# Four reorderings in a fused mixer and expert kernel: tokens' weights, half a modulation, filler products, gathered gates

## The chip, the cores and the metric

The kernel runs on one core of one Trainium2 chip. The metric is the device time in microseconds. Three runs of the kernel before gave 544.57, 546.89 and 544.63, so the median is 544.63.

## The reference, cut to what matters

One block of a modulated network on x of shape (4, 512, 512), all in float32:

```python
mod = (silu(c) @ wmod).reshape(4, 6, 1, -1)            # sa, ca, ga, sb, cb, gb per batch
h = layernorm(x) * (1 + ca) + sa
x = x + ga * attn(h)       # causal depthwise conv (4 taps), B/C/delta products, softplus,
                           # scan h_t = dA_t * h_(t-1) + Bu_t, output product, + D * conv
h = layernorm(x) * (1 + cb) + sb
logits = h @ w_router.T; probs = softmax(logits)       # 2 experts, every token goes to one
a = square(where(h@w_fc >= 0, h@w_fc, 0.5 * h@w_fc))
out = top_probability * (a @ w_proj of the chosen expert)
x = x + gb * out
```

## The kernel before, in words

There are two stages. The **mixer** (0 to about 148 us) works through four batches of 512 tokens, b = 0 to 3. The **expert stage** (to the end) works on the 2048 tokens sorted by expert in 17 blocks of 128 rows, which make up five units of 4, 4, 4, 3 and 2 blocks (`UNITS`; `FIRST` = 0, 4, 8, 12, 15 is the first block of each). It runs over eight blocks of hidden columns (`hb` = 0 to 7). Each engine has a queue of its own, written out by hand in program order, and semaphores tie them. No planner orders anything. So an instruction that waits holds up all that stands behind it on the same engine.

Batch b in the mixer, with the helpers of the code: VectorE takes the statistics of a row (`stats1`), ScalarE guesses the reciprocal root (`guess1`), VectorE mends it (`newton1`), ScalarE normalizes (`normalize1`). TensorE turns the rows over (`transposes1`, L1006), ScalarE multiplies and shifts on the way out of the accumulator (`modulate1`, L695) and starts the convolution (`last_tap`, L703). VectorE adds the other three taps (`conv`, L1359). TensorE computes `delta_product`, `C_product` (L1030), `B_product` (L1038), `state_product` (L1048) and `spread_delta` (L1024). ScalarE's `exp_minus_abs` (L711, L713) and `log_part` with VectorE's `softplus_residue` (L1368, L1370) and `softplus` make delta, and ScalarE's `decay` (L723, L725) copies it and exponentiates it. `scan` on VectorE (L1381 to L1388) needs delta, decay and the products. TensorE adds `skip_product` (L1063) and `state_output` (L1067), VectorE adds the residual (`residual`, L1397).

The second half of a batch is the router: `row_stats2` and `stats2` (statistics), `guess2` on ScalarE, `margin_products` on VectorE (four fused multiply-and-sum instructions, L1421, which raise `s_q`), `newton2`, `margins`. The last writes the mask `m1` (L1435), on which TensorE's `prefix` (L1072, L1073) and GpSimd's `candidates` (L555) wait, and the margin `al`, of which ScalarE takes the exponential (`margin_exp`, L744), behind the four instructions of `normalize2` (L739). One batch later, behind the scan, VectorE computes `ranks`, `permutations` (L1454) and `top_weight` of the batch before: two small instructions (L1458, L1461) that turn the exponential into each token's weight, 1 / (1 + e). GpSimd then scatters positions, tokens and weights of that batch to memory with four indirect transfers (L586). Before those it waits for `top_weight` (`s_tw`), and behind them stands its work on the next batch, `candidates` first. TensorE's `permuted_block` (L1091) and ScalarE's `place` (L777, L781) write the sorted rows.

In the expert stage TensorE multiplies without a break (L1180, L1201 for the first product, L1232 for the second) and VectorE accumulates. In its last block of columns, `hb` = 7, GpSimd does this in order: it gathers each row's `gb` gate (`gather_gb`, L598), adds x's own rows into blocks 8 to 16 (`add_own`, L605, each waiting for a block that VectorE has prepared, `s_pre`, L1678), waits until all those have landed, adds blocks 0 to 7 into the output (`add_rows`, L613) and stores blocks 8 to 16 (`put_rows`, L620). Each store waits for its block (`s_or`). The gates of blocks 4 to 7 (unit index 1) are needed by VectorE's `finish_rows(1)` (L1662). VectorE's last steps are `last_products` (L1686) and `last_sums` (L1693).

Of the kernel before, what the change touches and what calls it, by code (L numbers as in the profile page):

```python
# [35 lines left out]
TJ = L // P  # L36
# [3 lines left out]
UNITS = (4, 4, 4, 3, 2)  # L40
# [64 lines left out]
def build(nc, x, cT, wmod, wx, win, wout, conv_w, conv_b, A_log, Dvec, router_rows, wffn, out):  # L105
    with ExitStack() as ctx:
# [406 lines left out]
        def _(pool):  # L513
# [88 lines left out]
            def add_own(n):  # L602

                pool.wait_ge(s_pre, n - DIRECT + 1)
                pool.indirect_dma_start(out=acc[:, n, :], out_offset=None, in_=out,  # L605
                                        in_offset=bass.IndirectOffsetOnAxis(ap=sorted_meta[:, n, 1:2].bitcast(I32), axis=0),
                                        bounds_check=TOK - 1, oob_is_err=False, compute_op=ALU.add).then_inc(s_own[n - DIRECT], 16)
# [35 lines left out]
                add_own(n)  # L643

            pool.wait_ge(s_h[HM - 1], NU * (NHB - 1))
            for n in GATES[CH:]:
                gather_gb(n)
            for n in range(FIRST[3], NSUB):
                add_own(n)

            for n in range(NSUB - DIRECT):
                pool.wait_ge(s_own[n], 16)
# [7 lines left out]
        def _(act):  # L660
# [158 lines left out]
            mod_row_copy(4)  # L819
            normalize1(2)  # L820
            mod_row_copy(5)
            decay(1)
            guess2(0)
            modulate1(2, (0, 1))
            guess1(3)
            modulate1(2, (2, 3))
            last_tap(2, range(KT))
            normalize2(0)
            margin_exp(0)
# [123 lines left out]
        def _(pe):  # L953
# [112 lines left out]
            def state_output(b, j):  # L1066
                pe.matmul(out_bank[j][:, :], hs[:, P * j:P * j + P], woutg[b][:, :], start=False, stop=True).then_inc(s_y, 1)  # L1067

            def prefix(b):
                pe.wait_ge(s_m1, b + 1)  # L1070
                pe.wait_ge(s_x2, TJ * (b + 1))
                pe.matmul(pO[0][:, 0:TJ], before[:, :], m1[:, :], start=True, stop=True).then_inc(s_pf, 1)  # L1072
                pe.matmul(pO[0][:, TJ:2 * TJ], ones[:, :], m1[:, :], start=True, stop=True).then_inc(s_pf, 1)  # L1073
# [42 lines left out]
            for b in range(NB):  # L1116
# [44 lines left out]
                    transposes1(b + 2, (2, 3))  # L1161
                if b == 0:
                    delta_product(2)
                prefix(b)
            PARTS = ((0, 0), (0, 1), (1, 0))
            W, XS, A = (Whi, Wlo), (XShi, XSlo), (ahi, alo)
# [148 lines left out]
        def _(dve):  # L1315
# [253 lines left out]
            for b in range(NB):  # L1569
                nxt = b + 1 < NB  # L1570
                scan(b)
                if b == 0:
                    for n in range(NB):
                        out_weights(n)
                else:
                    ranks(b - 1)
                    permutations(b - 1)
                    if b == NB - 1:
                        assign_first()
                    top_weight(b - 1)  # L1580
                    if b == NB - 1:
                        prepare_rest()
                taps = {}
# [16 lines left out]
                if nxt:  # L1600
# [6 lines left out]
                    for n in range(TJ):  # L1607
                        row_stats2(b, n)
                stats2(b)
                if b == 0:  # L1610
                    router_row(False)
                    stats1(3)
# [65 lines left out]
                    dve.scalar_tensor_tensor(acc[:, n, :], acc[:, n, :], sorted_meta[:, n, 0:1], gb_row[n][:, :], ALU.mult,  # L1678
                                             ALU.mult).then_inc(s_pre, 1)

            def last_products(u, banks):
                for s in range(UNITS[u]):
                    n = FIRST[u] + s
                    dve.wait_ge(s_yy, NSUB * (NHB - 1) + n + 1)
                    dve.wait_ge(s_pre, n - DIRECT + 1)
                    dve.scalar_tensor_tensor(gb_row[n][:, :], yP[banks[s]][:, :], sorted_meta[:, n, 0:1], gb_row[n][:, :],  # L1686
                                             ALU.mult, ALU.mult).then_inc(s_yu, 1)
# [68 lines left out]
                low(NHB - 1, u)  # L1756
                finish_rows(u - 1)
            twice(1, NHB - 1, 3)
            last_products(2, range(WIDE))
            low(NHB - 1, 3)  # L1760
            last_sums(range(FIRST[2], FIRST[2] + 2))
            twice(1, NHB - 1, NU - 1)
            last_sums(range(FIRST[2] + 2, FIRST[3]))
            last_low()
            last_products(3, (0, 1, 2))
            last_sums(range(FIRST[3], FIRST[4]))
            last_products(4, (3, 0))
            last_sums(range(FIRST[4], NSUB))


# [33 lines left out]
```

## Time and profile before

| | |
|---|---|
| median of three runs | 544.63 us |
| the profiled execution, its own time | 547.68 us |
| its span, first to last instruction | 545.9 us |
| TensorE busy | 502.0 us, 92% of the span |
| VectorE busy | 345.7 us, 63% |
| ScalarE busy | 259.4 us, 48% |
| GpSimd busy | 158.4 us, 29% |
| mean granted TensorE clock | 0.958 |

The shares are averages over the two stages. The mixer takes a quarter of the span, and its work passes from engine to engine. The expert stage takes the rest, and nearly all of it is TensorE. What a reordering is worth has to be read inside its own stretch: in the timeline (one line for each run of equal instructions, with the idle time before it and what ended that) and in the windows (busy time of each engine in a stretch and the clock granted to TensorE).

### The profile page before, as it was taken

Reading aid. Unit: us, or ns where it says so; the run is one execution under the profiler, and the core shown is the slowest. Engines: PE = TensorE matmul, PEld = TensorE weight load, DVE = VectorE, ACT = ScalarE, POOL = GpSimd, SP = SyncE. Lnnn points to the kernel's source line nnn. Section 1 sums busy time; section 2 is a strip of 40 time slices with the busy share of each in tenths; the row PEclk is TensorE's granted clock in tenths of the full one; section 3 lists DMA queues with packets and bytes.
Section 4 is the critical chain, followed back from the end, with each engine's and each line's share of the span. In section 5 each row is a group of like instructions: output and inputs, shape, how many; then the busy total and the mean of one; then the engine's idle time right before and its main releaser. Section 6 shows DMA issues by size and latency. Waiting matters only on the chain.

```text
span 545.9 us, 7958 instructions
## 1 busy us (share of the span) xinstructions
PE 502.0 (92%) x2408; PEld 392.8 (72%) x2408; DVE 345.7 (63%) x730; ACT 259.4 (48%) x524; POOL 158.4 (29%) x204
## 2 busy tenths in 40 slices
PE   7899789987397999999999999999999999999990
PEld 1464365736276888898888888888888888988880
DVE  4579999699998575454445354545454534668781
ACT  1774295956785633443443354344345334433220
POOL 1100021122243510330150033034004304868673
PEclk9899969998697999999999999999999999999995
DMA  8931242220051004130022022002102300468692
GB/s 294 424 133 57 103 152 77 79 77 2 1 162 72 4 3 156 30 126 2 1 79 79 1 78 80 1 1 94 64 1 78 118 1 6 117 112 182 78 167 98
DMA packets 15730, 46.31 MB, mean 85 GB/s; under 512 B 5223, under 2 KB 5223, under 8 KB 12344
## 3 DMA queue, kind: packets, MB, share of 16 engines
q1 hardware_dynamic: 10600, 34.71, 17.9%
q0 software_dynamic: 5072, 10.79, 9.6%
q8 instruction: 41, 0.67, 0.5%
q14 instruction: 17, 0.14, 0.1%
HBM read 37.30 MB, written 8.71 MB: 84 GB/s over the span
## 4 chain that ended last, share of the span: by engine, by line
PE 75%; DVE 13%; ACT 4%; issue 3%; DMA 1%; ACTq 1%; POOL 1%; DVEq 0%; SPq 0%; POOLq 0%
PE bank L1232 34%; PE bank L1201 32%; DVE xc L1359 3%; ACT XSfull L777 2%; DVE st L1404 1%; DVE st L1341 1%; DMA x_in<-x 1%; PE bank L1030 1%; PE bank L1038 1%; DVE res L1397 1%; PE bank L1063 1%; PE bank L1006 1%; DVE eabs L1421 1%; PE bank L1067 1%; DVE hs L1387 1%
## 5 line engine op out<-in xcount | busy, mean ns | idle before, releaser
L569 POOL TENSOR_TENSOR Wlo<-raw,Whi (+1 forms) x60 | 76.6, 1307 | 228.0 <-ACT Whi L921 219.9
L1656 DVE TENSOR_TENSOR acc<-acc,bank 128x512 f32<-128x512 f32 x110 | 74.8, 687 | 57.2 <-PE bank L1232 57.2
L1232 PE MATMUL bank<-Whi,ahi 128*128 128x512 f32 x268 | 105.5, 394 | 4.3 <-DVE alo L1646 4.3
L1640 DVE TENSOR_TENSOR twice_h<-twice_h,bank 128x512 f32<-128x512 f32 (+2 forms) x80 | 48.2, 605 | 95.6 <-ACT twice_h L892 95.5
L1201 PE MATMUL bank<-XShi,Wlo 128*128 x304 | 108.1, 356 | 0.0
L1201 PE MATMUL bank<-XSlo,Whi 128*128 x304 | 108.0, 355 | 0.0
L1201 PE MATMUL bank<-XShi,Whi 128*128 x304 | 108.0, 355 | 0.0
L1232 PE MATMUL bank<-Wlo,ahi 128*128 128x512 f32 x268 | 105.5, 394 | 0.0
L1232 PE MATMUL bank<-Whi,alo 128*128 128x512 f32 x268 | 105.3, 393 | 0.0
L901 ACT ACTIVATE ahi<-twice_h 128x512 fp32r<-128x512 f32 (+2 forms) x78 | 44.6, 572 | 120.0 <-PE bank L1232 119.9
L892 ACT ACTIVATE twice_h<-bank 128x512 f32<-128x512 f32 (+2 forms) x78 | 41.4, 533 | 86.9 <-PE bank L1201 76.2
L1201 PEld LDWEIGHTS bank<-XSlo,Whi 128*128 128x128 f32 x304 | 57.3, 189 | 7.5
L1201 PEld LDWEIGHTS bank<-XShi,Whi 128*128 128x128 f32 x304 | 57.3, 189 | 7.5
L1201 PEld LDWEIGHTS bank<-XShi,Wlo 128*128 128x128 f32 x304 | 57.3, 188 | 6.8
L1232 PEld LDWEIGHTS bank<-Whi,ahi 128*128 128x128 f32 x268 | 51.0, 190 | 14.9 <-issue 4.7
L1232 PEld LDWEIGHTS bank<-Whi,alo 128*128 128x128 f32 x268 | 50.9, 190 | 10.8
L1232 PEld LDWEIGHTS bank<-Wlo,ahi 128*128 128x128 f32 x268 | 50.9, 190 | 10.2
L1646 DVE TENSOR_TENSOR alo<-a_full,ahi 128x512 fp32r<-128x512 f32 (+2 forms) x78 | 45.4, 612 | 0.0
L902 ACT ACTIVATE a_full<-twice_h 128x512 f32<-128x512 f32 (+2 forms) x78 | 43.3, 556 | 0.0
L1359 DVE SCALAR_TENSOR_TENSOR xc<-hT,cw,xc 128x512 f32<-128x512 f32 x48 | 33.6, 742 | 2.5 <-ACT xc L703 2.2
L777 ACT ACTIVATE XSfull<-bank,cols 128x128 f32 (+1 forms) x64 | 24.1, 460 | 20.0 <-PE bank L1091 17.7
L921 ACT ACTIVATE Whi<-raw 128x512 fp32r<-128x512 f32 x56 | 30.5, 616 | 0.0
(201 smaller groups left out, 570.1 us busy)
## 6 DMA issues: line engine op xcount, KB each, us to landing
raw<-wffn SPq DMA_DIRECT2D x16, 1024.0 KB, 5.1
wm<-wmod SPq DMA_DIRECT2D x6, 1024.0 KB, 12.8
out<-res SPq DMA_DIRECT2D x4, 1024.0 KB, 4.5
x_in<-x SPq DMA_DIRECT2D x3, 1024.0 KB, 12.4
ga_bc<-ga_rows SPq DMA_DIRECT2D x4, 256.0 KB, 3.7
x<-x SPq DMA_DIRECT2D x1, 1024.0 KB, 5.1
bc<-router_rows_scaled SPq DMA_DIRECT2D x4, 256.0 KB, 3.5
wx_sb<-wx SPq DMA_DIRECT2D x1, 514.0 KB, 8.6
```

The source lines that it names most:

```text
L569: pool.tensor_tensor(Wlo[:, hb % 2, c, :], raw[:, c, :], Whi[:, hb % 2, c, :].bitcast(F32), ALU.subtract).then_inc(s_wlo, 1)
L777: act.activation(XSfull[:, k, bass.ds(first, P)], place_bank[b][j][:, P * k:P * k + P], ACT.Identity, bias=cols[:, 4, k, b:b + 1], scale=c ...
L892: act.activation(twice_h[:, m, 0:w], hP[(par + u) % 2][m][:, 0:w], ACT.Relu).then_inc(s_relu[m], 1)
L901: act.activation(ahi[:, m, 0:w], twice_h[:, m, 0:w], ACT.Square, scale=0.5).then_inc(s_ah[m], 1)
L902: act.activation(a_full[:, m, 0:w], twice_h[:, m, 0:w], ACT.Square, scale=0.5).then_inc(s_af[m], 1)
L921: act.activation(Whi[:, 1 - par, c, :], raw[:, c, :], ACT.Copy).then_inc(s_whi, 1)
L1201: mm = pe.matmul(hP[(par + u) % 2][m][:, c0:c1], W[wp][:, par, 2 * e + k // 2, o:o + P], XS[xp][:, k, bass.ds(start_row[u] + c0, c1 - c0)] ...
L1232: mm = pe.matmul(yP[bank_of[s]][:, :], ahl[ap][:, m, P * s:P * s + P], W[wp][:, par, 4 + 2 * experts[s] + m, :], start=(m == 0 and n == 0) ...
L1359: ins = dve.scalar_tensor_tensor(xc[:, b % 2, k, :], hT[b % 2][:, k, tap:tap + L], cw[:, k, tap:tap + 1], xc[:, b % 2, k, :], ALU.mult, AL ...
L1640: dve.tensor_tensor(twice_h[:, m, 0:w], twice_h[:, m, 0:w], hP[(par + u) % 2][m][:, 0:w], ALU.add).then_inc(s_q2[m], 1)
L1646: dve.tensor_tensor(alo[:, m, 0:w], a_full[:, m, 0:w], ahi[:, m, 0:w].bitcast(F32), ALU.subtract).then_inc(s_al2[m], 1)
L1656: dve.tensor_tensor(acc[:, n, :], acc[:, n, :], yP[s][:, :], ALU.add).then_inc(s_yu, 1)
```

## The change

```diff
@@ GpSimd, last block of columns
             pool.wait_ge(s_h[HM - 1], NU * (NHB - 1))
-            for n in GATES[CH:]:
+            for n in range(1, FIRST[1]):
                 gather_gb(n)
             for n in range(FIRST[3], NSUB):
                 add_own(n)
+            assert GATES[CH - 1:] == tuple(range(DIRECT))
+            for n in range(FIRST[1], DIRECT):
+                gather_gb(n)
@@ ScalarE
             mod_row_copy(5)
+            modulate1(2, (0, 1))
+            guess2(0)
             decay(1)
-            guess2(0)
-            modulate1(2, (0, 1))
+            modulate1(2, (2, 3))
             guess1(3)
-            modulate1(2, (2, 3))
             last_tap(2, range(KT))
@@ TensorE
+            def keep_rate(b, count):
+                pe.wait_ge(s_q, TJ * b + 2)
+                pe.wait_ge(s_x2, TJ * (b + 1))
+                for n in range(count):
+                    pe.matmul(pO[1][:, :], ident[:, :], wout_sb[:, :], start=True, stop=True)
...
                 if b == 0:
                     delta_product(2)
+                    keep_rate(b, 3)
+                if b == 2:
+                    keep_rate(b, 2)
                 prefix(b)
@@ VectorE
                     if b == NB - 1:
                         assign_first()
-                    top_weight(b - 1)
                     if b == NB - 1:
                         prepare_rest()
...
                 stats2(b)
+                if b > 0:
+                    top_weight(b - 1)
                 if b == 0:
@@ VectorE, the end
-            last_products(3, (0, 1, 2))
-            last_sums(range(FIRST[3], FIRST[4]))
-            last_products(4, (3, 0))
+            last_products(3, (0, 1, 2), (0, 1))
+            last_sums((FIRST[3],))
+            last_products(3, (0, 1, 2), (2,))
+            last_sums((FIRST[3] + 1, FIRST[3] + 2))
+            last_products(4, (3, 0), (0, 1))
             last_sums(range(FIRST[4], NSUB))
```

`last_products` gets a third argument, the rows of the unit that it works on; the call for unit 2 passes all four. The products of `keep_rate` are 128 x 128 by 128 x 512 in float32, and nothing reads what they write.

## Rows read from the trace of the kernel before

**Rows 1.** The head of the page.

```profile
span 545.9 us, 7958 instructions
```

**Rows 2.** VectorE's waits, 0 to 170 us: total, times, longest.

```profile
DVE den L1458 <- ACT eal L744: 2.9, 1, 2.9
```

**Rows 3.** Timeline, batch 1's scan and after: start, duration, instruction, [idle before <-releaser].

```profile
93.55 1.50 ACT L777 ACTIVATE XSfull<-bank,cols 128x128 f32 x4 [2.76 <-PE bank L1091]
...
98.80 0.58 ACT L723 ACTIVATE delta<-bank 128x512 f32<-128x512 f32 x1
...
99.41 0.69 DVE L1381 TENSOR_TENSOR eabs<-delta,bank 128x512 f32<-128x512 f32 x1 [1.42 <-ACT delta L723]
...
107.10 0.26 ACT L711 ACTIVATE eabs<-bank 128x128 f32<-128x128 f32 x1
107.23 0.17 DVE L1458 TENSOR_SCALAR den<-eal 128x4 f32<-128x4 f32 x1 [2.93 <-ACT eal L744]
...
107.43 0.18 DVE L1461 RECIPROCAL meta<-den 128x4 f32<-128x4 f32 x1
...
110.15 0.22 DVE L1368 TENSOR_SCALAR w<-eabs 128x128 f32<-128x128 f32 x1
```

**Rows 4.** Timeline of TensorE, 68 to 89 us.

```profile
68.42 1.33 PE L1006 MATMUL bank<-ident,z 128*128 128x128 f32 x8 [2.44 <-ACT hT L695]
...
73.31 0.59 PE L1072 MATMUL bank<-m,before 128*128 128x4 f32 x2 [1.90 <-DVE m L1435]
...
74.18 5.47 PE L1063 MATMUL bank<-diag,xc 128*128 128x128 f32 x24
...
85.08 3.60 PE L1030 MATMUL bank<-hT,wx_sb 128*128 128x512 f32 x8
```

**Rows 5.** Windows: stretch, busy of PE, PEld, DVE, ACT, POOL, then PEclk.

```profile
69.50:71.00 1.50, 1.50 (x35) 0.91 (x33) 1.31 (x6) 1.50 (x3) 0.00 (x0) 0.69 1.26 392
```

**Rows 6.** Timeline of GpSimd after batch 0's token weights.

```profile
108.38 1.46 POOL L586 DMA_INDIRECT sorted_rows<-meta,posI  x1 [4.24 <-issue]
...
113.74 0.21 POOL L574 COPY meta<-tokbat 128x8 int32<-128x8 int32 x1
```

**Rows 7.** Timeline, batch 2's mask and batch 3's first residual.

```profile
127.16 0.39 PE L1072 MATMUL bank<-m,before 128*128 128x4 f32 x2 [2.82 <-DVE m L1435]
...
134.19 0.69 DVE L1397 TENSOR_TENSOR res<-bank,x 128x512 f32<-128x512 f32 x1
```

**Rows 8.** The chain that ended last: start, us, what.

```profile
167.32 8.16 PE bank L1232 x24
...
180.92 5.44 PE bank L1232 x24
```

**Rows 9.** Timeline of GpSimd, 488 us to its last transfer.

```profile
488.50 1.00 POOL L598 DMA_INDIRECT gb_row<-gb_rows,sorted_meta  x1 [0.30 <-issue]
...
497.56 1.57 POOL L605 DMA_INDIRECT acc<-out,sorted_meta  x1 [0.30 <-issue]
...
511.17 1.59 POOL L613 DMA_INDIRECT out<-acc,sorted_meta  x1 [4.35 <-DMA acc<-out,sorted_meta]
...
526.84 1.03 POOL L620 DMA_INDIRECT out<-acc,sorted_meta  x1 [0.30 <-issue]
...
537.83 0.98 POOL L620 DMA_INDIRECT out<-acc,sorted_meta  x1 [0.30 <-issue]
```

**Rows 10.** The 17 gate gathers, line L598.

```profile
DMA to landing us min/median/max: 3.7/4.4/6.9
```

**Rows 11.** Timeline of VectorE in the last block of columns.

```profile
492.46 3.39 DVE L1678 SCALAR_TENSOR_TENSOR acc<-acc,sorted_meta,gb_row 128x512 f32<-128x512 f32 x5
...
514.22 2.73 DVE L1662 SCALAR_TENSOR_TENSOR acc<-acc,sorted_meta,gb_row 128x512 f32<-128x512 f32 x4
...
523.63 1.29 DVE L1693 TENSOR_TENSOR acc<-acc,gb_row 128x512 f32<-128x512 f32 x2
...
532.80 1.28 DVE L1693 TENSOR_TENSOR acc<-acc,gb_row 128x512 f32<-128x512 f32 x2
```

More of the change, by code:

```diff
@@ L1679, in prepare_rows, with last_products @@
                                              ALU.mult).then_inc(s_pre, 1)
-            def last_products(u, banks):
-                for s in range(UNITS[u]):
+            def last_products(u, banks, rows):
+                for s in rows:
                     n = FIRST[u] + s
@@ L1758, in _ @@
             twice(1, NHB - 1, 3)
-            last_products(2, range(WIDE))
+            last_products(2, range(WIDE), range(WIDE))
             low(NHB - 1, 3)
```

## The prediction, made before the changed kernel ran

> **What bounds the kernel now.** I read the page, then the chain that ended last, then VectorE's waits, then the timeline of the two stretches that the diff touches. The page gives the span, 545.9 us [rows 1]; the profiled execution took 547.68, 1.8 more, and the median of the runs is 544.63, 3.05 below it. From 167 us on the chain of waits is TensorE in runs of 24 products, 5.44 us each [rows 8], up to its last product near 531.7. Nothing in the diff touches that, so the middle of the kernel only moves with what lies ahead of it. Two stretches are left.
>
> In the mixer the bound is VectorE: it has work almost without a gap from 40 to 167 us, and what counts are its few waits. The longest one that the diff touches is 2.9 us for ScalarE's exponential [rows 2]. The timeline shows its place: behind batch 2's scan and ranks, `top_weight(1)` starts at 107.23 after 2.93 us of idling, and the convolution of batch 3 stands behind it. A second wait, 1.42 us, is for delta at 99.41 [rows 3].
>
> At the end the bound is not VectorE or TensorE, whatever the chain says, but GpSimd's queue. VectorE's last sum ends at 532.80 + 1.28 = 534.1 [rows 11]; GpSimd issues its last store at 537.83, with only the fixed 0.30 us of issue before each [rows 9]. That stream of 17 transfers runs without a real gap from 511.17, and there it had waited 4.35 us for the own rows to land.
>
> **The change part by part.**
>
> *Tokens' weights behind the next statistics.* In the loop's step b = 2 the two instructions leave a place where they waited. Removed there: 2.93 us of waiting and 107.61 - 107.23 = 0.38 us of work. Both instructions come back behind `stats2`, with the exponential long there, so the 0.38 is gained up to that point and given back after it. In b = 1 and b = 3 there was no wait and only the 0.38 moves. In b = 3 it is gained for what counts: between the old place and the new one stand `prepare_rest`, the residual at 134.19 [rows 7] and `stats2(3)`, whose result releases ScalarE's last `guess2`, two `place` blocks behind it and with them the start of the expert stage.
>
> *What is late next.* Without the wait VectorE starts the four taps at once and wants `exp_minus_abs(3)` behind them, which ended at 107.10 + 0.57 = 107.7 (two short instructions) [rows 3]. VectorE's taps would end at 110.15 - 2.93 - 0.38 = 106.8. So if ScalarE keeps its times the new wait is 0.9 and the gain at that point 110.15 - 107.75 = 2.4. It is 3.3 if ScalarE is earlier by 0.9 or more.
>
> *Filler products and half a modulation.* These are what makes ScalarE earlier. TensorE idled 2.44 us before 68.42 because it needed ScalarE's modulation, and 1.90 before 73.31 for the mask. Its clock fell to 1.2 GHz between those (0.69 mean in 69.5 to 71.0 [rows 5]) and the 24 short products of L1063 took 5.47 us [rows 4]. At full clock they take half of that, 2.7. So 2.7 us, with the outputs behind them about 3.0, are lost by TensorE from 74 on, and it works without a gap from there to 98. ScalarE waits for it at 93.55 (2.76 us for a permuted block [rows 3]) and runs without a gap from there to 98.80, 13.6 us in all to 107.10. With the modulation's first half in the free time before 66.02, the transposes of the second half follow at 66.0 rather than 68.4, `delta_product(2)` ends near 69.2, and three fillers follow. One float32 product of 512 columns is two of the eight records in 3.60 us, so 0.9, three cost 2.6 and end at 71.8, before the mask at 73.3: no cost. The gap left is 1.5. I take it that the clock holds: two gaps of 2.44 and 1.90 close together brought it down, and one of 1.5 is less than either; the lower end is that it falls as before. Then TensorE's permuted block comes 3 us sooner, `guess2(1)` follows VectorE's statistics, `decay(2)` goes from 98.80 to about 95.9, the 1.42 wait disappears, and ScalarE is 2.9 early at 107.10, so no new wait. Mixer gain: 1.42 + 2.93 + 0.38 = 4.7. If the fillers do nothing: 2.4. If the modulation delays a decay: it cannot, `decay(1)` waits for TensorE until 66.02 anyway; the two instructions (1.43) and `guess2(0)` (0.4) fit ahead of it.
>
> The two fillers of b = 2 (1.7 us) lie in the 2.82 us before 127.16 [rows 7]. At this place VectorE reaches its residual at 134.19 some 1 us after TensorE has delivered, so a full clock gives it nothing; it lets ScalarE place two blocks in time for the shift by 4.7. Worth 0 alone, at the least -0.2 if they overrun the mask.
>
> *GpSimd in the mixer.* The four scatters of a batch now come behind `stats2`, in front of `candidates` of the next batch. From the weights at 107.61 to the next copy at 113.74 they take 6.1 us [rows 3, 6]. In b = 1 `stats2` ends at 93.1: the candidates come at 93.1 + 6.1 + 0.8 = 100.0; `ranks` wants them at 102.71 - 1.4 = 101.3. Slack 1.3, and 1.0 in b = 2 (weights at 117.9, candidates 124.9, ranks 126.0). Cost 0; two slow transfers, 0.5 each more, would still fit.
>
> *Start of the expert stage.* The first run of 24 products took 8.16 instead of 5.44, because TensorE had idled and was at the low clock: 2.7 lost [rows 8]. It idles as long in the new kernel. Where in its run the clock comes back I can't tell, so 0, with both ends: between 1 us less and 1 us more.
>
> *Gates of blocks 4 to 7 later.* Seven gathers took 488.50 to 497.56, 1.3 each, then five own rows 1.87 each to 506.8, then the wait to 511.17 [rows 9]. Now three gathers end at 492.4. The first own row waits for VectorE: 492.46 + 0.68, and 0.8 from there to the transfer (as from 107.61 to 108.38 [rows 3, 6]), so 493.9. Five: 503.2. Four gathers: 508.5. The own rows, landed at 508 at the latest (506.8 - 503.2 = 3.6 before 511.17 - 0.6), no longer delay. The 17 transfers start at 508.8, 2.3 earlier. `finish_rows(1)` at 514.22 needs the gates: the last is issued at about 507.4 and lands 3.7 to 6.9 later [rows 10], 511.1 to 514.3. No cost. But the stream now meets VectorE: the first store, 526.84 - 2.3 = 524.5, needs a sum that ends at 523.63 + 0.65 = 524.3 and starts 0.8 later, 525.1. So 1.7 remain. The split of `last_products(3)` puts block 12's sum at 529.7 rather than 530.4, against a store wanted at 530.5: it saves 0.8 that the shift would otherwise have lost again. The last store can't be before 534.1 + 0.8 = 534.9 and comes by the stream at 536.1. Tail gain 1.7; bounds 0 (if transfers and not issues hold the stream) and 2.9 (537.83 - 534.9).
>
> **Sum.** 4.7 + 1.7 + 0 = 6.4 on the profiled execution: 547.68 to 541.3. The median lies 3.05 lower. If the timed runs are like the profiled one but for a constant, that gives 538.2. If the clock did not fall at 70 us in the timed runs, the 1.42 wait was not there, and 5.0 remain: 539.6. I take the middle, 539.0.
>
> The Trainium skill ("TensorE: Matmul & The Clock Gate", Part 1) says that the point at which the clock changes is not tied to the kernel's start and differs from run to run. By that rule the second of these two readings holds in part of the runs, and the fillers are worth nothing in those: it speaks for 539.6. The spread of the three runs, 2.3 us, goes with it; a single trace can't show it.
>
> **Rivals.**
> - *ScalarE takes over as the bound.* The clock falls anyway (the gaps before 73.3 are not filled tightly enough) or was never low in timed runs and something else holds ScalarE. For: ScalarE has no idle time from 93.55 to 107.7 [rows 3]. Against: 3 us of slack come with the clock. The mixer gives 2.4, the tail 1.7: 544.6 - 4.1 = 540.5.
> - *The tail gives nothing.* The transfers themselves hold the stream and not their issue, so a burst that starts earlier ends no earlier. For: the eight adds are (526.84 - 511.17) / 8 = 1.96 apart. Against: the stores behind them are (537.83 - 526.84) / 8 = 1.37 apart, little over one issue of 0.98 and 0.30 [rows 9]. 544.6 - 4.7 = 539.9, and with the rival above 542.2, which is within 0.5% of before.
> - *Slower: the gates come too late.* `finish_rows(1)` stands ahead of VectorE's next `twice`, which releases TensorE's next products. If the four gathers land behind the own rows' adds, every us past 514.3 is one us of TensorE. It turns the sum of 6.4 negative only if the last lands later than 520.7, 13 us after its issue; the worst seen is 6.9 [rows 10]. At 16 us it would give 544.6 + 2.7 = 547.3.
> - *The weights' scatters hold `ranks`*: each us over the slack of 1.0 to 1.3 costs one us in each of two batches; at 1.5 us over, 539.0 + 3 = 542.
>
> **How the numbers follow.** Forecast, by its two readings 538.2 and 539.6: 0.28 and 0.27. ScalarE bound, 540.5: 0.18. No tail gain, 539.9: 0.10. Both, or the scatters over their slack, 542 to 544: 0.13. Slower: 0.04. The range takes the first four to 542.2 and downwards the 1 us of the expert stage's start and the tail's 2.9: 536.8. The measurement can tell 0.5%, 2.7 us, from no change: under 541.9 is faster, 0.82; same 0.14; slower 0.04.
>
> **What would show it.** In the changed profile: no wait of VectorE at L1458; `exp_minus_abs(3)` without a VectorE wait at L1368 (wrong if some 0.9 stands there); a full clock from 69 to 138 us; L1063 x24 in about 2.7 us; no wait for delta at L1381; L1442 with no wait for `cand`; the start of L1232 near 162.6; GpSimd's first L613 about 2.3 earlier relative to TensorE's last product, its last L620 about 1.7. The prediction is wrong if the first L1232 comes less than 2 us earlier, or if a wait for a gate shows at L1662.

## The result: 542.8 against 546.2 us, faster, by less than forecast

In the first comparison, on one chip, the changed kernel took 542.8 us in the median of 9 runs (541.03 to 543.46), the kernel before 546.18 (9 runs, 544.57 to 549.05). The ratio is 0.9936, 95% interval 0.9913 to 0.9959. A second comparison on another chip gave 542.41 (540.36 to 543.07) against 545.8, ratio 0.9928, interval 0.9907 to 0.9949. So 3.4 us are gained, faster by 0.6%. The forecast was 539.0 with a range up to 542.2: the direction was right, the time is 0.6 us outside the range. The starting point moved too: the forecast counted from 544.63, the median of three runs of the kernel before, and its nine runs here have 546.18. One execution of a later experiment (fill_order_gates_back) took 865.4 us at a granted clock of 0.559, and its ratio is without it.

The profiled execution of the changed kernel took 543.34 (span 541.6, mean granted clock 0.969), that of the kernel before 547.68 (span 545.9): 4.3 less where 6.4 were forecast. First VectorE and ScalarE around batch 1's scan (timeline, as [rows 3]):

```profile
96.38 0.58 ACT L727 ACTIVATE delta<-bank 128x512 f32<-128x512 f32 x1
...
98.36 0.68 DVE L1395 TENSOR_TENSOR eabs<-delta,bank 128x512 f32<-128x512 f32 x1
...
104.68 0.26 ACT L715 ACTIVATE eabs<-bank 128x128 f32<-128x128 f32 x1
105.97 0.22 DVE L1382 TENSOR_SCALAR w<-eabs 128x128 f32<-128x128 f32 x1
```

L1395 is the old L1381 and L1382 the old L1368. Delta stood at 98.80 and stands at 96.38; VectorE wanted it at 98.3 and no longer waits. The weights' two instructions and their wait of 2.93 have left this place, and the taps end at 105.97 instead of 110.15. ScalarE's two instructions that they need next were finished 0.7 us earlier (at 105.29), so no new wait took the place of the old one.

TensorE (timeline, as [rows 4]; L1078 are the unread products):

```profile
66.26 1.04 PE L1010 MATMUL bank<-ident,z 128*128 128x128 f32 x8
...
69.56 2.84 PE L1078 MATMUL bank<-wout_sb,ident 128*128 128x512 f32 x6
73.76 0.39 PE L1083 MATMUL bank<-m,before 128*128 128x4 f32 x2 [1.36 <-DVE m L1449]
74.23 2.97 PE L1067 MATMUL bank<-diag,xc 128*128 128x128 f32 x24
```

The transposes are 2.2 earlier with no wait ahead of them, the two gaps of 2.44 and 1.90 have become one of 1.36, and the 24 short products take 2.97 instead of 5.47. The mask itself is 0.44 later than before, since the whole execution entered this stretch 0.44 later. The first projection of the expert stage and the last transfers (chain of waits, then GpSimd's timeline, as [rows 8, 9]):

```profile
163.92 8.50 PE bank L1246 x24
```

```profile
506.01 1.62 POOL L613 DMA_INDIRECT out<-acc,sorted_meta  x1 [0.30 <-issue]
...
522.07 1.04 POOL L620 DMA_INDIRECT out<-acc,sorted_meta  x1 [1.17 <-DVE acc L1708]
...
533.48 0.98 POOL L620 DMA_INDIRECT out<-acc,sorted_meta  x1 [0.30 <-issue]
```

The projection starts 3.40 earlier and its first run takes 0.34 longer; TensorE's last product is 3.06 earlier (528.24 against 531.30). The wait of 4.35 ahead of the first L613 is gone, and one of 1.17 for VectorE's sum stands ahead of the first L620. The last store comes 4.35 earlier: 5.24 after TensorE's last product instead of 6.53, so the tail (from TensorE's last product to the last store) gave 1.29. In all the profiled execution gained 3.40 at the projection, less 0.34 in its first run, plus 1.29 in the tail: 4.35.

### The profile page after: what moved, and what is told of

It is laid out like the page before. It is cut to its first block, busy times and chain, and to the rows that moved or that the text cites. A ratio compares the mean times of both kernels' runs of the same rounds, so it can differ in the third digit from the quotient of the medians.

```text
span 541.6 us, 7980 instructions
## 1 busy us (share of the span) xinstructions
PE 501.2 (93%) x2418; PEld 390.0 (72%) x2418; DVE 346.4 (64%) x730; ACT 259.8 (48%) x524; POOL 159.3 (29%) x204
## 4 chain that ended last, share of the span: by engine, by line
PE 71%; DVE 18%; issue 4%; ACT 3%; DMA 1%; ACTq 1%; DVEq 0%; POOL 0%; SPq 0%; POOLq 0%
PE bank L1246 34%; PE bank L1215 33%; DVE xc L1373 4%; DVE st L1418 2%; DVE res L1411 2%; DVE st L1355 1%; DMA x_in<-x 1%; DVE eabs L1435 1%; DVE hs L1401 1%; ACT XSfull L781 1%; PE bank L1194 1%; PE bank L1034 1%; PE bank L965 1%; PE bank L1052 1%; PE bank L1042 1%
## 5 line engine op out<-in xcount | busy, mean ns | idle before, releaser
L586 POOL DMA_INDIRECT sorted_rows<-meta,posI x16 | 16.8, 1050 | 50.7 <-issue 50.7
```

Source lines behind the costliest of these rows:

```text
L586: pool.indirect_dma_start(out=meta_dram, out_offset=bass.IndirectOffsetOnAxis(ap=posI[:, b % 2, j:j + 1], axis=0), in_=meta[:, b % 2, j, : ...
```

## The experiments

All kernels compute the whole reference. Each comparison has the kernel before on the same chip; medians of different chips are not compared with each other.

**The kernel before, a second time.**

> The kernel before, unchanged, run as a kernel of its own, to see another trace of it and its spread. Theory A (the forecast's error was that I carried a fixed 3.05 us from the profiled execution to the median): the executions of this same program differ by 2 to 4 us, and a trace of a fast one (about 544.6) shows the TensorE clock full near 70 to 80 us, L1063 x24 in about 3.0 instead of 5.47 us and no 1.42 us wait for delta at L1381. Theory B (the profile was typical and single parts of the change give less when timed): the trace looks as before, clock low from 70 to 80, and all times lie within 1 us of each other.

Measured: 545.91 (544.68 to 549.26), ratio 1.0011 (0.9982 to 1.004). Its profiled execution (548.62, clock 0.957) shows the same waits as the first, 2.9 at L1458 and 1.4 at L1381. Its twelve executions are of two kinds: eight of 544.7 to 546.2 at a clock of 0.960 to 0.969, four of 548.5 to 549.3 at 0.957. Both profiles of the kernel before caught the low-clock one. So the distance from profile to median depends on which kind the profile caught, and that reopened the last step of the prediction.

**The tokens' weights at their old place.**

```diff
+                    top_weight(b - 1)
...
-                if b > 0:
-                    top_weight(b - 1)
```

> The changed kernel with the tokens' weights back at their old place, right behind the ranks. Theory A: with the products' clock kept, ScalarE delivers the exponential at 104.6, VectorE reaches it at 103.3, so the wait returns at about 1.4 us and with the 0.3 of work the mixer is 1.7 us longer: 544.5 against the changed kernel's 542.8. Theory B (the wait removed was the 2.93 of the old trace whatever else changed): 3.3 us longer, 546.1, as slow as the kernel before.

Measured: 542.96 (540.38 to 545.46), ratio 0.9945 (0.9915 to 0.9976). The wait is back (VectorE's timeline):

```profile
98.17 0.68 DVE L1395 TENSOR_TENSOR eabs<-delta,bank 128x512 f32<-128x512 f32 x1
...
105.82 0.17 DVE L1472 TENSOR_SCALAR den<-eal 128x4 f32<-128x4 f32 x1 [2.77 <-ACT eal L748]
...
108.75 0.22 DVE L1382 TENSOR_SCALAR w<-eabs 128x128 f32<-128x128 f32 x1
```

From L1395 to L1382 it is 10.58 us against 7.61 in the changed kernel, 2.97 more, and 2.03 of it are left at the first projection (165.95 against 163.92). But the two profiles don't differ in this part alone. This one has the unread products and the gap of 1.35 behind them as the changed kernel has, and still its clock fell between 73 and 79 us (the window has 0.72), and the 24 short products took 4.51 instead of 2.97:

```profile
73.56 0.39 PE L1083 MATMUL bank<-m,before 128*128 128x4 f32 x2 [1.35 <-DVE m L1449]
...
74.03 4.51 PE L1067 MATMUL bank<-diag,xc 128*128 128x128 f32 x24
```

Where the clock is full there, in the profiles of fill_tw_back and fill_order_tw_back below, the wait is 1.85 and 1.86 and L1395 to L1382 takes 9.67 and 9.66. So this part is worth 2.06 at that point at a full clock, and the 2.97 hold some 0.9 of the clock. The ratio is only 0.0009 (0.5 us) above the changed kernel's: four of the twelve executions took 540.4 to 540.8 at a clock of 0.977. Something pays out in some executions and not in others, as large as the part itself.

**No unread products.**

```diff
-                    keep_rate(b, 3)
-                if b == 2:
-                    keep_rate(b, 2)
```

> The changed kernel without the five unread products. Theory A: the clock falls near 70 us in part of the executions, and in those batch 1 runs 2.4 to 3 us later on TensorE and VectorE waits 1 to 2 us more; in the others nothing is lost. Median 1 us longer, 543.8, spread wider. Theory B: the modulation ahead of the decay alone keeps TensorE busy enough, 542.8.

Measured: 545.15 (543.35 to 546.15), ratio 0.9983 (0.9957 to 1.0009), the clock 0.956 to 0.966 in all executions. TensorE and VectorE's waits:

```profile
66.06 1.04 PE L1010 MATMUL bank<-ident,z 128*128 128x128 f32 x8
...
73.55 0.59 PE L1083 MATMUL bank<-m,before 128*128 128x4 f32 x2 [4.13 <-DVE m L1446]
74.43 4.72 PE L1067 MATMUL bank<-diag,xc 128*128 128x128 f32 x24
```

```profile
DVE w L1379 <- ACT eabs L717: 0.8, 1, 0.8
```

With the modulation moved alone the two gaps join into one of 4.13, the clock falls in it, the products take 4.72, and VectorE meets a late exponential: 0.8, the size that the prediction gave for that case (0.9). The rest of the change without this part gives 0.2%, in an interval that includes no change. This is the rival "ScalarE takes over as the bound", made to happen.

**Unit 2's gates in the old order.**

```diff
-            for n in range(1, FIRST[1]):
+            for n in GATES[CH:]:
...
-            for n in range(FIRST[1], DIRECT):
-                gather_gb(n)
```

> The changed kernel with all seven gates gathered ahead of the own rows, as before. Theory A: GpSimd waits some 4.3 us again for the own rows, the last 17 transfers start 2.1 us later relative to TensorE's last product, the last store 1.3 us later: 544.1. Theory B (the transfers and not their issue set the end): 542.8, and the last store lands as far behind TensorE's last product as in the changed kernel, 13.3 us from 528.24 to the end.

Measured: 544.13 (541.74 to 545.17), ratio 0.9965 (0.994 to 0.9989). In its profile the last L620 starts at 533.07 and the last product at 526.49, 6.58 apart, against 5.24 in the changed kernel and 6.53 in the kernel before. The tail's part is 1.3. The median is no measure of it here: it depends on the mix of executions, which spread over 3.4 us.

**Unread products wherever TensorE idles ahead of the expert stage.** Eight more around the last prefix sums, four ahead of the first projection, to take the clock out of the comparison; then the same with one part of the change taken back, and on the kernel before.

```diff
+                if b == NB - 1:
+                    pe.wait_ge(s_x2, TJ * NB)
+                    for n in range(6):
+                        pe.matmul(pO[1][:, :], ident[:, :], wout_sb[:, :], start=True, stop=True)
...
+                if b == NB - 1:
+                    for n in range(2):
+                        pe.matmul(pO[1][:, :], ident[:, :], wout_sb[:, :], start=True, stop=True)
...
+            for n in range(4):
+                pe.matmul(place_bank[NB - 1][0][:, :], ident[:, :], wout_sb[:, :], start=True, stop=True)
```

> The changed kernel with 12 more unread products: six before the last prefix, two behind it (TensorE waits 6.7 and 2.3 us there) and four before the first second-product of the expert stage (4.0 us). Theory A (where the clock falls differs from execution to execution, and that is what spreads the runs and what my sum left out): the clock stays full from 10 us to the last product, the first 24 products of L1246 take 5.44 instead of 8.5 us, the first product of the expert stage 1.85 instead of 3.77, and the median falls by 3 to 5 us to 538 to 540 with a spread under 1 us. Theory B (the spread has another source, such as when the first loads land): the median falls by no more than 3 and the spread of some 2.5 us stays.

> As fill_both, with the tokens' weights back at their old place. With the clock held in every wait only this step differs. Theory A (the trace's wait of 2.8 us for the exponential is real and on the path): 2.0 us slower than fill_both, as the first second-product came at 165.95 against 163.92 in the two traces. Theory B (timed runs say it gives nothing: 542.96 against 542.8): equal to fill_both within 0.5 us.

> As fill_both, with the gates gathered in the old order. Theory A: 1.3 us slower than fill_both, since GpSimd's stream of the last 17 transfers starts 2.1 us later and VectorE takes back 0.8. Theory B (transfers set the end): equal.

> The kernel before with all unread products (those of the change and the twelve of fill_both) and nothing else of the change. Theory A: the clock costs the kernel before up to 8 us in its slow executions and 3 in its fast ones; this gives 542.5 with a spread under 1 us, and the rest of the change (weights 2.0, gates 1.3, the modulation 0.5) is what lies between it and fill_both, 3.8 us. Theory B: the fillers give the kernel before less than 1.5 us, 544.5 or more.

Measured: fill_both 543.7 (543.4 to 545.17), ratio 0.9981 (0.996 to 1.0002); without the weights' move 544.51, 0.9995 (0.9972 to 1.0018); without the gates' move 545.04, 1.0003 (0.998 to 1.0025); the kernel before with all unread products 545.59, 1.0022 (1.0 to 1.0045). The clock rose to 0.974 to 0.988 and ten of fill_both's twelve executions lie within 0.6 us, so in this kernel the clock carried most of the spread. But a higher clock made the kernel no faster. Where it went is in GpSimd's and VectorE's groups, 149 to 165 us (busy us, mean ns, idle before). First the changed kernel:

```profile
L569 POOL TENSOR_TENSOR Wlo<-raw,Whi 128x512 fp32r<-128x512 f32 x4 | 5.5, 1406 | 8.3 <-ACT Whi L760 8.3
L1637 DVE TENSOR_TENSOR XSlo<-XSfull,XShi x4 | 3.6, 961 | 0.5 <-issue 0.5
```

then fill_both:

```profile
L569 POOL TENSOR_TENSOR Wlo<-raw,Whi 128x512 fp32r<-128x512 f32 x4 | 6.3, 1617 | 6.2 <-ACT Whi L760 6.2
L1648 DVE TENSOR_TENSOR XSlo<-XSfull,XShi x4 | 6.6, 1705 | 0.5 <-issue 0.5
```

VectorE's four low halves take 1705 ns each instead of 961. GpSimd's four, also a subtraction of two operands from the SBUF, run beside them and rise from 1406 to 1617. The first projection of fill_both came at 166.94, behind 3.67 us of unread products, against 163.92. The new theory: the two engines slow each other when both work on two SBUF operands, and work that arrives earlier falls into the overlap. (One more trace of this batch bears on the clock: in fill_gates_back the 24 short products took 4.58 in spite of the unread products ahead of them, as in tw_back.)

**The overlap forbidden.** GpSimd's halves wait until VectorE's of batch 2 are written: one line, added to fill_both, to the changed kernel, and to fill_both with a part taken back.

```diff
+                    pool.wait_ge(s_xlo, KT * 2)
                     pool.wait_ge(s_wlo, CH // 2)
                     for c in range(CH // 2, CH):
```

> The twelve further unread products stay, and GpSimd's low halves of batch 2's second group of blocks (L569, x4) wait until VectorE's low halves of batch 2 (L1648, x4) are written. Theory A (the two engines slow each other when both work on two operands in the SBUF): the group L1648 falls from 6.6 us to about 2.5, the first token projection comes about 4.1 us earlier than the 166.7 of the same kernel without the order, near 162.6, and the median is about 543.7 - 4.1 = 539.6. Theory B (VectorE's low halves are late for another reason, and GpSimd's halves are themselves needed at once): L1648 keeps over 4 us or L569 ends later by as much as L1648 gains, the first projection stays near 166.7, and the median stays within 0.8 of 543.7.

> The changed kernel with that one order added (GpSimd's L569 x4 behind VectorE's L1637 x4 of batch 2), no further unread products. Theory A: L1637 takes 2.5 us instead of 3.6, the first projection comes about 1 us earlier than 163.9, the median is about 541.7, and the spread between executions with a high and a low granted clock stays. Theory B: nothing is gained or up to 1 us is lost, since GpSimd's halves end later: 542.8 to 543.8.

> As fill_order, but the token weights are found ahead of the statistics again (the old place). If the clock and the order are settled by the two additions, the difference to fill_order is what that part of the change is worth by itself: the exponential wait of 2.8 comes back ahead of the statistics (L1382 of the changed kernel), less what the idle engine did in it, so +2.0 by the shift of the first projection in the changed kernel and the one without this part (163.92 against 165.95). If the part's value is hidden by a transfer or by ScalarE, +0.5 or less.

> As fill_order, but unit 2's gates are gathered ahead of the rows again (the old order). Theory: the tail's 1.3 us (4.35 of L613's and L620's shift less 3.06 of PE's last product) come back, +1.3 over fill_order. Rival: the tail is set by the last GpSimd rows whatever the gathers do, +0.4 or less.

Measured, all on one chip (the kernel before 543.57): fill_order 540.64 (539.5 to 542.69), ratio 0.9937 (0.9909 to 0.9965); order_only 540.8 (538.84 to 542.19), 0.9939 (0.9911 to 0.9967); fill_order_tw_back 541.97, 0.9955 (0.9934 to 0.9976); fill_order_gates_back 541.6, 0.9958 (0.9935 to 0.9981). The groups in fill_order, the second one VectorE's over a window with three more of them:

```profile
L569 POOL TENSOR_TENSOR Wlo<-raw,Whi 128x512 fp32r<-128x512 f32 x4 | 5.0, 1294 | 9.1 <-DVE XSlo L1649 9.1
L1649 DVE TENSOR_TENSOR XSlo<-XSfull,XShi x7 | 4.4, 685 | 0.5 <-issue 0.5
```

685 and 1294 ns each alone, 1705 and 1617 together: theory A. The first projection is at 163.06 instead of 166.94, 3.9 earlier as expected (4.1; 0.4 of it was gained ahead of this stretch, so 3.4 are the order's), and against the kernel before the same unread products give 0.6% instead of 0.2%. The Trainium skill ("GPSIMD Engine Reference", 1. Specifications) lists the SBUF interfaces as shared with VectorE, with contention for instructions with two SBUF inputs. By that rule these two groups must meet, and the traces agree; the page has no price, and here it is 1.0 us per VectorE instruction of 128x512 and 0.3 per GpSimd instruction.

With the order settled the parts can be read between kernels of one chip: the weights' move 1.33 (expected 2.0), the gates' move 0.96 (expected 1.3). No interval was taken of these two differences, and the ranges overlap. For the directions stands that fill_order's four fastest executions (539.5 to 539.9) lie 1 us below the fastest of either kernel with a part taken back (540.99, 540.97). The 2.0 came from profiles with different clocks, as said above.

The clock isn't settled, though. fill_order's other four executions took 541.4 to 542.7, at 0.977 to 0.986 instead of 0.987 to 0.990. That these are a kind of their own is likely and not shown: fill_order's profile is of a fast one. But the profile of fill_order_tw_back caught a slower execution (543.15, clock 0.984), and in it the eight records of the four unread products ahead of the projection took 5.37 instead of 3.67 us, as in the profile of fill_tw_back. The chain that ended last shows them there:

```profile
161.28 5.37 PE bank L1324 x8
```

So the products that were to keep the clock full ran in part at the low one themselves, and the projection waited for them.

**The last four.** To separate what was still open: the changed kernel again; the combination that the runs pointed to (the eight products around the last prefix sums and the order); the order on the kernel before; and the modulation alone taken back, whose edit stands here. The order is the same line, now behind the wait for `s_wlo`.

```diff
-            modulate1(2, (0, 1))
-            guess2(0)
...
-            modulate1(2, (2, 3))
+            guess2(0)
+            modulate1(2, (0, 1))
...
+            modulate1(2, (2, 3))
```

> The changed kernel unchanged, as the measure for the three others on this chip. Theory: its median stays 2.5 to 3.5 under the kernel before, and its executions spread over 4 us with the granted clock, from about 540.5 at 0.977 to 545 at 0.965.

> The changed kernel with eight of the unread products around the last prefix sums (none ahead of the first projection) and with GpSimd's L569 x4 behind VectorE's low halves of batch 2. Theory A (both engines slow each other, and the four products ahead of the projection delay it: in fill_order it began at 163.06 behind 3.67 of them, in order_only at 162.17 without): the projection begins near 161.5 at the full clock, the median is 3 under after_again and the spread under 2 us. Theory B (the order alone gives all of it): as order_only, 2 under after_again, and no less spread.

> The kernel before with GpSimd's L569 x4 behind VectorE's low halves of batch 2, nothing of the change. In the kernel before one of the four instructions L1622 took 1.79 instead of 0.68, so theory A expects 1.1 us less in executions with a low clock there and up to 4 us less in those with a high one: a median 1 to 2 under the kernel before. Theory B (the overlap matters only once the change has moved the work): under 0.5.

> The changed kernel with batch 2's modulation in its old place (both halves behind the decay, the guess ahead of it). By the prediction's step the delta wait of 1.42 ahead of L1395 comes back and every later row of the mixer is about 1.4 later: +1.4 over after_again. Rival: the delta wait is given back by the idle time that the token weights left, which now lies behind it, and 0.5 or less is seen.

Measured, one chip (the kernel before 545.8, 29 runs): after_again 542.41 (540.36 to 543.07; a spread of 2.7 where 4 was expected), 0.9928 (0.9907 to 0.9949); fill_first_order 541.31 (540.64 to 541.71), 0.992 (0.9891 to 0.9949); before_order 544.03 (542.53 to 547.07), 0.9986 (0.996 to 1.0013); mod_back 543.0 (541.56 to 543.37), 0.9951 (0.9931 to 0.997).

- before_order's median is lower, but not its kinds of execution: at a clock of 0.967 it takes 542.9 to 543.6 and the kernel before 543.0 to 543.4; at 0.958 it is 547.0 against 547.1 to 547.8. The order is worth 0 to 0.5 there, theory B, though the median is 1.8 lower by its mix. In the kernel before one of the four low halves is slowed, and they take 3.60 us together; in before_filled (the same kernel at a full clock) they take 5.77, in fill_both 6.59, and behind the order 2.50. So what the overlap costs depends on when the two groups meet.
- mod_back: 0.6, not 1.4; near the rival's size, with ranges that overlap. See below.
- fill_first_order lies 1.1 under the changed kernel on the same chip, and its spread is 1.1 instead of 2.7, but it has six executions only, and the ranges and the intervals against the kernel before overlap. That it beats the changed kernel isn't shown. Its projection came at 162.40 where 161.5 was expected, and at the low clock: without the four products ahead of it the first 24 took 8.30.

**The trace that settles the first term** is before_order's, because its profile caught a high-clock execution (543.0, clock 0.967). Up to 150 us it is the kernel before. TensorE's timeline and VectorE's:

```profile
68.25 1.88 PE L1007 MATMUL bank<-ident,z 128*128 128x128 f32 x8 [2.44 <-ACT hT L696]
73.15 0.39 PE L1073 MATMUL bank<-m,before 128*128 128x4 f32 x2 [1.18 <-DVE m L1436]
73.62 2.96 PE L1064 MATMUL bank<-diag,xc 128*128 128x128 f32 x24
```

```profile
97.76 0.68 DVE L1382 TENSOR_TENSOR eabs<-delta,bank 128x512 f32<-128x512 f32 x1
...
104.50 0.17 DVE L1459 TENSOR_SCALAR den<-eal 128x4 f32<-128x4 f32 x1 [1.86 <-ACT eal L745]
...
107.43 0.22 DVE L1369 TENSOR_SCALAR w<-eabs 128x128 f32<-128x128 f32 x1
```

Here the clock fell already at the transposes (they take 1.88 instead of 1.33) and was back before the mask. The 24 products take 2.96, no wait for delta exists, and the exponential is waited for 1.86, not 2.93. How long the clock stays low in each is in the windows. before_order:

```profile
68.00:73.00 5.00, 3.71 (x40) 2.83 (x40) 4.19 (x22) 4.78 (x10) 0.00 (x0) 0.66 0.88 300
73.00:79.00 6.00, 5.85 (x34) 4.49 (x35) 5.79 (x20) 6.00 (x11) 1.18 (x5) 1.00 0.24 98
```

and the profiled execution of the kernel before:

```profile
72.00:74.00 2.00, 0.69 (x4) 0.69 (x4) 1.79 (x10) 2.00 (x4) 0.66 (x3) 0.50 0.95 352
74.00:79.00 5.00, 5.00 (x24) 5.00 (x25) 4.83 (x17) 5.00 (x9) 0.51 (x3) 0.50 0.09 31
```

Of the kernel before's 29 executions on this chip 12 are low-clock executions (547.1 to 547.8, all at 0.958), 4 took 543.0 to 543.4 at 0.967 to 0.970, and 13 lie between. Of the changed kernel's twelve, four took 540.4 to 541.2 at 0.971 to 0.974 and eight 542.0 to 543.1.

## Why the prediction was wrong

**What held.** The mixer's mechanism, step by step: no wait at the weights, none for delta, none for `cand` (candidates ended ahead of the ranks at 101.81), L1067 x24 in 2.97 (forecast 2.7), the full clock from 69 to 123 us (0.92 in 123 to 138, which the forecast had at full). At L1382 4.18 were gained by the clock of the trace and 4.62 from the mask on, where 4.7 were forecast. The case of the failing clock gave a new wait of 0.8 for a forecast 0.9 (no_fill). The gates were never late: L1677 started at 511.16 without a wait. One reading was loose without harm: ScalarE isn't without a gap from 93.55 on, it has 0.49 at 96.63, and as much in the changed kernel.

The miss is 542.8 - 539.0 = 3.8 us. About half of it lies in the step from profile to median and half in the sum for the profiled execution (6.4 forecast, 4.35 measured).

**The step that failed first** is the one that goes from the profiled execution to the median. It took the 3.05 us between them as a constant, or left out only the 1.42 of delta in its second reading, and so put the changed kernel's median 2.3 below its profile (541.3 to 539.0); it was 0.54 below. The 3.05 itself was chance: against the median of nine runs the same profile lies 1.5 above. The profiled execution of the kernel before is a low-clock one, in which the clock is low from 70 to 80 us. In before_order's high-clock one delta isn't waited for at all and the exponential 1.86 us, 1.07 less. So the mixer's term there is not 4.7 but 1.86 + 0.38 = 2.2, and from mask to taps the traces say the same: before_order 107.43 - 72.92 = 34.51, the changed kernel 105.97 - 73.53 = 32.44, 2.1 less.

**The mixer's term doesn't arrive whole.** This is the larger part of what is missing in the profiled execution. The forecast took the gain at the taps for the gain at the expert stage. In fact VectorE's first mask to its last mask (L1435, L1436, L1460 and L1449 below are the same statement) shrinks by 4.13 at the low clock and by 1.62 at the high one:

| kernel, clock near 70 to 79 us | first mask | last mask | between |
|---|---|---|---|
| the kernel before, low | 73.09 | 144.96 | 71.87 |
| before_order, back before the mask | 72.92 | 142.26 | 69.34 |
| fill_tw_back, full | 73.23 | 142.59 | 69.36 |
| fill_order_tw_back, full | 73.31 | 142.64 | 69.33 |
| no_fill, low | 73.33 | 142.14 | 68.81 |
| the changed kernel, full | 73.53 | 141.27 | 67.74 |
| mod_back, back before the mask | 72.82 | 140.61 | 67.79 |

```profile
144.96 0.17 DVE L1435 TENSOR_SCALAR m<-lg 128x4 f32<-128x4 f32 x1
```

```profile
142.26 0.17 DVE L1436 TENSOR_SCALAR m<-lg 128x4 f32<-128x4 f32 x1
```

```profile
142.59 0.17 DVE L1460 TENSOR_SCALAR m<-lg 128x4 f32<-128x4 f32 x1
```

```profile
141.27 0.24 DVE L1449 TENSOR_SCALAR m<-lg 128x4 f32<-128x4 f32 x1
```

Part of the difference to 4.62 and 2.1 is the work of the two weight instructions, which the new place puts ahead of each mask again; the forecast counted their 0.38 in full. From the last mask to the projection the changed kernel then takes 22.65, the kernel before 22.36, before_order 21.25, order_only 21.60. So at the projection 3.84 are left at the low clock (counted from the first mask; 3.40 by the time of the trace) and 1.3 between before_order and order_only, 163.51 and 162.17. With the tail's 1.3, and less the 0.34 of the first run at the low clock, that is 4.8 and 2.6. The timed executions agree, if the ends of the two lists above answer to each other: 547.5 to 542.7 (4.8) and 543.2 to 540.8 (2.4). The median lies between, 3.4. The forecast subtracted the gain of a low-clock execution from a median near the high-clock ones.

**The tail's term was mis-sized.** 1.7 forecast, 1.29 came. From the last product to the last L620 it is 6.52 to 6.58 us in five profiles with the old order (7.81 in before_again, where one store took 2.13), and 5.23 or 5.24 in every profile with the new one. The first L620 did come 1.7 earlier relative to TensorE's last product, as forecast; the eight steps behind it took 11.41 instead of 10.99, mostly because one of them held the queue for 1.37 instead of 1.01.

**The start of the expert stage** was forecast at 0, "between 1 us less and 1 us more". Its first 24 products took 8.50 in the changed kernel's profile and 7.37 in after_again's, against 8.16, inside these ends. With the order it went beyond them: 5.75 in order_only's profile. There (538.84) the clock is full:

```profile
162.17 5.75 PE bank L1247 x24
```

and that execution ends where the forecast was, by a gain that the forecast didn't have in its sum: luck, not confirmation. The windows around it, 160 to 163 and 163 to 169 us:

```profile
160.00:163.00 3.00, 0.91 (x5) 0.70 (x5) 2.93 (x10) 3.00 (x7) 0.00 (x0) 1.00 0.83 311
163.00:169.00 6.00, 6.00 (x28) 4.96 (x27) 6.00 (x10) 3.22 (x7) 4.67 (x5) 1.00 0.05 11
```

**Which part did what.** The weights' move alone gives the 1.6 of the high-clock rows in the table: fill_tw_back has the unread products and the new modulation and is no faster between the masks than before_order, which has neither. Those two parts give at a low clock only, 2.5 together (71.87 to 69.36). Without the unread products the table shows 1.07 more and the ratio is 0.9983. They don't always hold the clock: of the twelve profiles with them and the new modulation it fell behind them in two (4.51 in tw_back, 4.58 in fill_gates_back, 2.97 in the others). What the modulation's move does beside them isn't shown. With the products and the old modulation (mod_back) the gap of 2.44 is back, and still no wait for delta, in a profile in which the clock fell at 68 and was back at 73:

```profile
68.15 1.97 PE L1010 MATMUL bank<-ident,z 128*128 128x128 f32 x8 [2.44 <-ACT hT L699]
71.65 2.84 PE L1078 MATMUL bank<-wout_sb,ident 128*128 128x512 f32 x6
74.33 0.28 PE L1083 MATMUL bank<-m,before 128*128 128x4 f32 x2
```

There the products overrun the mask by 1.3 (released at 72.86, run at 74.33), and nothing behind it minds. In before_filled it did matter: there the products ran in part at the low clock (3.83), the mask's own products came at 75.11, and between the masks it is 70.36, 1.0 more than in before_order.

**The weight of the two readings.** The prediction drew on the rule of the Trainium skill ("TensorE: Matmul & The Clock Gate", Part 1) that the point at which the clock changes differs from run to run, which spoke for its second reading, 539.6, and still took the middle of the two, 539.0. The low-clock and the high-clock executions bear it out, and it deserved the whole weight: it reaches the exponential's wait as well as delta's.

**What stays open.** Why the clock fell behind the unread products in two profiles of twelve. What sets the first mask, which stands at 73.53 in one profile of the changed kernel and at 74.42 in the other, and moves all behind it. Why three of after_again's slower executions (542.6 to 543.1) have its highest clock, 0.977. And where the 0.3 comes from by which both moves measure less than their rows (1.33 against 1.62, 0.96 against 1.3), which the spread of the executions could hide.

## What to carry to other kernels

Ask which kind of execution the profile caught before a gain read from it is subtracted from a median: a wait that exists only at a low clock is worth nothing in the runs at a full one, and a second profile of the same kernel with another mean clock tells it. Unread products that bridge a gap are an insurance at best: they gave nothing where the clock held anyway, failed to hold it in two profiles of twelve, and the four ahead of the projection ran in part at the low clock themselves in two profiles of seven. And look at what the earlier work runs into: here VectorE and GpSimd, each with two SBUF operands, gave back 3.4 us until one wait put them behind each other. A part is best priced where everything random ahead of it is pinned, on one chip, and by the distance between two instructions: one ahead of its stretch, and one at the place where the gain has to arrive, not where it arises.

## What the runs showed of the hardware

- Two subtractions of 128x512 with both operands in the SBUF, on VectorE and GpSimd at once: 685 to 1705 ns and 1294 to 1617 ns. Four of each took 6.9 us side by side (151.14 to 158.03 in fill_both) and take 2.7 + 5.2 = 7.9 one behind the other, so the overlap is no loss in sum; it is a loss for whoever waits for VectorE's half (3.4 us at the projection), and no engine's wait for GpSimd's shows in either trace.
- A gap of 4.13 us took TensorE's clock down (24 products in 4.72 us); with one of 1.36 behind three unread products (six records) it stayed up in ten profiles (2.97) and fell in two (4.51, 4.58). With gaps of 2.44 and 1.2 to 1.9 the work of the kernel before had it low from 68 to 73 us in one profile (before_order) and from 70 to 80 in two.
- The executions of the kernel before fell into kinds by the mean granted clock, 0.958, 0.964 and 0.967 to 0.970, with about 547.5, 544.7 and 543.2 us: 4.3 us between executions of one program. In the changed kernel the clock doesn't order them so (540.9 at 0.972, 543.1 at 0.977).
